# Sharing the second biases of 59 expert visits between TensorE and VectorE, with wider gate operations and an identity product for the residual

## What is computed

```python
xn = layernorm(x)                                    # x: (8, 256, 128)
# attention
Qf, Kf = elu(xn @ Wq) + 1, elu(xn @ Wk) + 1          # 16 heads of 8 features
num = Qf @ (Kf.T @ V);  den = Qf @ sum(Kf) + 1e-6    # V = xn @ Wv, by batch and head
attention = (num / den) @ Wo
# experts
probs = softmax(xn @ gate_w.T + gate_b)              # 8 logits
topk_vals, topk_idx = top_k(probs, 2)
h = relu(xn @ w1[e] + b1[e])                         # 128 -> 256
expert_out = h @ w2[e] + b2[e]                       # 256 -> 128
ffn = sum over the two of topk_vals * expert_out
out = x + attention + ffn
```

## Time and profile before

| | us |
|---|---|
| median of 3 runs (119.38 to 120.27) | 119.73 |
| the profiled execution | 119.96 |
| its span, first to last instruction | 118.2 |
| around the span | 1.76 |
| TensorE busy | 100.9 (85% of the span) |
| VectorE busy | 71.0 (60%) |
| ScalarE busy | 58.4 (49%) |
| GpSimd busy | 50.8 (43%) |

### The profile page before, as it was taken

One profiled execution on the slowest core, in us unless ns is written; L12 is line 12 of the kernel. 1 busy time (PEld: TensorE's weight loads), 2 busy tenths in 40 slices (PEclk: granted clock), 3 DMA queues, 4 the chain that ended last, 5 costly groups with the idle time before them and its releaser, 6 DMA issues.

```text
span 118.2 us, 3075 instructions
## 1 busy us (share of the span) xinstructions
PE 100.9 (85%) x763; PEld 91.3 (77%) x763; DVE 71.0 (60%) x291; ACT 58.4 (49%) x167; POOL 50.8 (43%) x66
## 2 busy tenths in 40 slices
PE   6967989999797897579999999999999899999100
PEld 6935968667676786469999999999999799999100
DVE  0749897998718976320575656557566565574600
ACT  1556996454020111117667676667666476666000
POOL 5004800467777778011001404022514458787870
PEclk9999999999999999967999999999999999999955
DMA  3999000002112116999855655856677758882522
GB/s 94 237 322 392 32 0 6 0 0 72 51 48 72 48 53 153 240 246 377 240 129 134 148 140 152 181 143 133 177 176 153 171 107 185 177 152 22 44 22 25
DMA packets 16656, 15.52 MB, mean 131 GB/s; under 512 B 1920, under 2 KB 16256, under 8 KB 16512
## 3 DMA queue, kind: packets, MB, share of 16 engines
q1 hardware_dynamic: 13248, 12.88, 38.8%
q0 software_dynamic: 2816, 2.18, 11.8%
q10 hardware_dynamic: 576, 0.27, 0.9%
HBM read 12.09 MB, written 3.23 MB: 130 GB/s over the span
## 4 chain that ended last, share of the span: by engine, by line
issue 28%; POOL 19%; PE 19%; DVE 13%; DMA 10%; ACT 2%; SPq 2%; POOLq 2%; DVEq 0%
POOL out L459 19%; DMA x_tok<-in_x 6%; DMA out<-res 5%; PE banks L968 4%; PE banks L937 3%; PE banks L1030 3%; PE banks L990 3%; PE banks L1005 2%; DVE att L766 2%; POOLq L115 2%; DVE rden L762 1%; SPq L354 1%; PE banks L921 1%; DVE idx L634 1%; PE banks L967 1%
## 5 line engine op out<-in xcount | busy, mean ns | idle before, releaser
L547 ACT ACTIVATE h<-banks,w_now 128x128 f32<-128x128 f32 x118 | 36.9, 364 | 19.7 <-PE banks L1061 19.7
L459 POOL DMA_INDIRECT out<-acc,token x16 | 25.0, 1562 | 34.5 <-DVE acc L795 33.3
L1061 PE MATMUL banks<-xsT,w_now 128*128 x236 | 37.5, 283 | 0.1
L1074 PE MATMUL banks<-w_all,h 128*128 x236 | 36.2, 277 | 0.3 <-DVE y L787 0.2
L1061 PEld LDWEIGHTS banks<-xsT,w_now 128*128 128x128 f32 x236 | 31.9, 197 | 0.8 <-issue 0.5
L787 DVE TENSOR_TENSOR y<-banks,w_all 128x128 f32<-128x128 f32 x59 | 17.2, 292 | 24.1 <-PE banks L1074 15.6
L1074 PEld LDWEIGHTS banks<-w_all,h 128*128 128x128 f32 x236 | 30.9, 192 | 1.0 <-issue 0.9
L795 DVE SCALAR_TENSOR_TENSOR acc<-y,xs,acc 128x128 f32 x59 | 20.7, 351 | 0.8 <-DVE y L787 0.5
L444 POOL DMA_INDIRECT sorted_dram<-xrow,slot x16 | 15.8, 990 | 5.3 <-issue 4.6
L893 PE MATMUL banks<-ones 128*128 128x128 f32 x42 | 7.9, 355 | 1.1 <-POOL ones L387 1.1
L893 PEld LDWEIGHTS banks<-ones 128*128 128x128 f32 x42 | 7.4, 265 | 1.5 <-POOL ones L387 1.1
(11 more groups left out here) (97 smaller groups left out, 108.7 us busy)
## 6 DMA issues: line engine op xcount, KB each, us to landing
w_now<-in_w1b SPq DMA_DIRECT2D x59, 129.0 KB, 2.5
w_all<-in_w SPq DMA_DIRECT2D x1, 1536.0 KB, 9.6
out<-res SPq DMA_DIRECT2D x4, 256.0 KB, 5.4
xs<-sorted_dram SPq DMA_DIRECT2D x3, 276.0 KB, 5.4
x_tok<-in_x SPq DMA_DIRECT2D x3, 256.0 KB, 6.6
xs<-sorted_dram SPq DMA_DIRECT2D x2, 138.0 KB, 3.4
x_tok<-in_x SPq DMA_DIRECT2D x2, 128.0 KB, 2.6
sorted_dram<-xrow,slot POOLq DMA_INDIRECT x16, 2.4
```

The lines of the kernel that those rows point to most:

```text
L459: nc.gpsimd.indirect_dma_start(out=out_rows, out_offset=bass.IndirectOffsetOnAxis(ap=token[:, s:s + 1], axis=0), in_=acc[:, s * D:(s + 1) ...
L547: nc.scalar.activation(h[:, i % NH, c, :], h_ps[i % NHP][:, c * P:(c + 1) * P], ACT.Relu, bias=w1_now[:, i % NW, H + c:H + c + 1]).then_in ...
L1061: last = nc.tensor.matmul(h_ps[i % NHP][:, c * P:(c + 1) * P], w1_now[:, i % NW, c * P:(c + 1) * P], xsT[:, bass.ds(toff, P)], start=True, ...
L1074: last = nc.tensor.matmul(y_ps[i % NYP], h[:, i % NH, c, :], w2_all[:, bass.ds(woff + c * D, D)], start=(c == 0), stop=(c == KC - 1))
```

## The change

- Second biases. `bias_by_pe(i)` is true for odd visits and the last four, 31 of 59. In these `second_product` starts with a product of three rows of ones (bf16) with three rows that hold b2 split into three bf16 parts; `take_y` is left out and `accumulate` reads PSUM. Other visits stay as they were. GpSimd makes the three parts (`split_b2`, five operations on 8 partitions), SyncE lays them out.
- Wider operations. Logits are taken for four tiles at a time, the pairs found for tiles 0 to 7, 8 to 11 and 12 to 15 (three groups, not four), the early gates made for eight tiles at once; kf of the first block comes after the first row numbers. The order on TensorE changes with it.
- Residual. `project_out(k)` starts with the product of the identity with x (fp32, 512 columns) into the same bank; ScalarE copies the sum out (`copy_sum`), VectorE's `residual` goes.
- Fillers. Four products stand between the last `project_out` and the first `transpose_rows`; one of the three fillers at the front goes.
- wq and the gate's bias are loaded by SyncE and no longer by ScalarE's queue; b2 is loaded once more by itself.

```diff
+    EARLY, LATE = slice(0, 8), slice(8, T)
+    PAIR_GROUPS = [(0, 8), (8, 12), (12, 16)]
...
+        def bias_by_pe(i):
+
+            return i % 2 == 1 or i >= NI - 4
...
+            sp.dma_start(gate_bias[:], gate_b.partition_broadcast(P)).then_inc(gate_b_in, 16)
+            sp.dma_start(wq_f[:], wq).then_inc(wq_in, 16)
+            sp.dma_start(b2_f[:], b2).then_inc(b2_in, 16)
             sp.dma_start(w2_all[:], w2).then_inc(w2_in, 16)
+            sp.wait_ge(b2_step, 5)
+            for j in range(3):
+                sp.dma_start(b2_split[j:j + 1, :].rearrange("o (e c) -> o e c", c=WROW)[:, :, 0:D],
+                             b2_parts[j][:]).then_inc(b2_placed, 16)
...
+            def split_b2():
+
+                pool.wait_ge(b2_in, 16)
+                nc.gpsimd.tensor_copy(b2_parts[0][:], b2_f[:]).then_inc(b2_step, 1)
...
+            def copy_sum(k):
+
+                act.wait_ge(wo_done, k + 1)
+                nc.scalar.copy(res[:, blk_tiles(k), :], wo_ps[k].rearrange("p (t d) -> p t d", t=4)).then_inc(res_done, 1)
...
+            copy_attT(0)
+            copy_attT(1)
+            copy_sum(0)
+            copy_attT(2)
+            copy_sum(1)
+            copy_attT(3)
+            copy_sum(2)
             copy_xsT(0)
+            copy_sum(3)
...
-            def residual(k):
-                dve.wait_ge(wo_done, k + 1)
-                nc.vector.tensor_tensor(res[:, blk_tiles(k), :], wo_ps[k].rearrange("p (t d) -> p t d", t=4),
-                                        x_tok[:, blk_tiles(k), :], ALU.add).then_inc(res_done, 1)
...
             def accumulate(i, toff, goff):
-                dve.wait_ge(y_done, i + 1)
+                if bias_by_pe(i):
+                    dve.wait_ge(l2_done, i + 1)
+                    share = y_ps[i % NYP]
+                else:
+                    dve.wait_ge(y_done, biases_by_dve(i + 1))
...
-                nc.vector.scalar_tensor_tensor(out=mine, in0=y[:, i % 2, :], scalar=xs[:, bass.ds(goff, 1)], in1=mine,
+                nc.vector.scalar_tensor_tensor(out=mine, in0=share, scalar=xs[:, bass.ds(goff, 1)], in1=mine,
...
             top_two(0)
+            top_two(1)
             take_logits(1)
-            top_two(1)
+            top_two(2)
+            top_two(3)
             find_pair(0)
             take_logits(2)
-            top_two(2)
+            top_two(4)
+            top_two(5)
+            find_pair(1)
+            take_logits(3)
+            top_two(6)
+            top_two(7)
+            find_pair(2)
+            shares()
             choose(0)
-            take_logits(3)
-            top_two(3)
-            find_pair(1)
-            choose(1)
-            take_logits(4)
-            top_two(4)
-            take_logits(5)
-            top_two(5)
-            find_pair(2)
-            take_logits(6)
-            top_two(6)
-            take_logits(7)
-            top_two(7)
-            find_pair(3)
-            shares(0)
-            shares(1)
             late_shift()
-            finish_k(0)
             pair_starts()
             places(1, slice(0, 4))
+            finish_k(0)
+            finish_k(1)
             places(2, slice(4, T))
-            finish_k(1)
             mask_kv(0)
             finish_q(0)
-            choose(2)
-            choose(3)
+            choose(1)
...
-                if i == 0:
+                if i == 0 and not bias_by_pe(0):
                     take_y(0, woffs[0][0])
-                if i + 1 < NI:
+                if i + 1 < NI and not bias_by_pe(i + 1):
                     take_y(i + 1, woffs[(i + 1) // LOADS][(i + 1) % LOADS])
...
+                for i in range(parts_with(4 * k), parts_with(4 * k + 3) + 1):
+                    pe.wait_ge(x_in[i - 1], 16)
+                nc.tensor.matmul(wo_ps[k].rearrange("p (t d) -> p t d", t=4), ident_t[:], x_tok[:, blk_tiles(k), :],
+                                 start=True, stop=False)
                 pe.wait_ge(attT_copied, k + 1)
                 for j in range(4):
                     t = 4 * k + j
                     last = nc.tensor.matmul(wo_ps[k][:, j * P:(j + 1) * P], attT[:, t * P:(t + 1) * P], wo_f[:],
-                                            start=True, stop=True)
+                                            start=False, stop=(j == 3))
                 last.then_inc(wo_done, 1)
...
+                elif bias_by_pe(i - NYP):
+                    pe.wait_ge(acc_done, i - NYP + 1)
                 else:
-                    pe.wait_ge(y_done, i - NYP + 1)
+                    pe.wait_ge(y_done, biases_by_dve(i - NYP + 1))
+                if bias_by_pe(i):
+                    pe.wait_ge(b2_placed, 16 * 3)
+                    nc.tensor.matmul(y_ps[i % NYP], ones_bf[0:3, 0:P], b2_split[:, bass.ds(woff, D)],
+                                     start=True, stop=False)
                 for c in range(KC):
                     last = nc.tensor.matmul(y_ps[i % NYP], h[:, i % NH, c, :],
                                             w2_all[:, bass.ds(woff + c * D, D)],
-                                            start=(c == 0), stop=(c == KC - 1))
+                                            start=(c == 0 and not bias_by_pe(i)), stop=(c == KC - 1))
                 last.then_inc(l2_done, 1)
 
...
-            warm_up(3)
+            warm_up(2)
             project_vg(2)
+            project_vg(3)
             transpose_x(3)
-            project_vg(3)
+            project_vg(4)
             transpose_x(4)
+            project_vg(5)
             rank_rows(0)
-            project_vg(4)
-            rank_rows(1)
-            project_vg(5)
             project_vg(6)
             project_vg(7)
+            rank_rows(1)
             project_k(1)
+            project_q(0)
             rank_rows(2)
-            project_q(0)
-            rank_rows(3)
             project_k(2)
...
+            warm_up(4, residuals=3)
             transpose_rows(0)
             transpose_rows(1)
```

More of the change, by code:

```diff
@@ L129, in linear_attention_with_pair_sorted_experts @@
         wo_f = sb("wo_f", [P, D])
+        b2_f = sb("b2_f", [E, D])
+        b2_rest = sb("b2_rest", [E, D])
+        b2_parts = [sb(f"b2_part{j}", [E, D], BF16) for j in range(3)]
+        b2_split = sb("b2_split", [3, E * WROW], BF16)
         gate_bias = sb("gate_bias", [P, E])
@@ L204, in linear_attention_with_pair_sorted_experts @@
         q_ps = [banks[:, i, :] for i in (2, 3, 4, 0)]
[L205 to L206 removed]
+        vg_four = [banks[:, i:i + 2, 0:R * (D + E)].rearrange("p b (r n) -> p b r n", r=R) for i in (2, 6, 2, 6)]
+        k_ps = [banks[:, i, :].rearrange("p (t d) -> p t d", t=4) for i in (4, 1, 0, 7)]
         rank_ps = banks[:, 5, 0:(T + 1) * NP].rearrange("p (t c) -> p t c", c=NP)
@@ L324, in normalised, with biases_by_dve, pairs_known @@
             return [sum(len(n) for n in norm[:i + 1]) for norm in (NORM_DVE, NORM_ACT, NORM_POOL)]
+        def bias_by_pe(i):
+            return i % 2 == 1 or i >= NI - 4
+        def biases_by_dve(i):
+            return sum(not bias_by_pe(j) for j in range(i))
+        def pairs_known(t):
+            return sum(t >= a for a, _ in PAIR_GROUPS)
         def group_of_visit(i):
@@ L569, in _ @@
             exp_gates(0)
-            exp_gates(1)
             exp_k(0)
-            for b in range(4, 7):
+            for b in range(4, 6):
                 copy_v(b)
             exp_k(1)
+            copy_v(6)
             copy_v(7)
             exp_q(0)
+            exp_gates(1)
             exp_k(2)
-            exp_gates(2)
             exp_q(1)
@@ L582, in _ @@
             exp_q(3)
-            for k in range(NBLK):
-                copy_attT(k)
+            copy_attT(0)
[5 more added lines that the diff above has]
+            copy_sum(2)
             copy_xsT(0)
+            copy_sum(3)
             for i in range(NI):
@@ L865, in _ @@
             dve.wait_ge(w2_in, 16)
-            residual(3)
             dve.wait_ge(acc_set, 1)
@@ L887, in _, with warm_up @@
         def _(pe):
-            def warm_up(times, after=0):
+            def warm_up(times, after=0, residuals=0):
                 pe.wait_ge(ones_set, 1)
@@ L949, in rank_rows @@
                 pe.wait_ge(pair_done, g + 1)
-                nc.tensor.matmul(rank_ps[:, blk_tiles(g), :], before_bf[:], of_pair[:, blk_tiles(g), :],
-                                 start=False, stop=False)
-                for t in range(4 * g, 4 * g + 4):
+                a, b = PAIR_GROUPS[g]
+                nc.tensor.matmul(rank_ps[:, a:b, :], before_bf[:], of_pair[:, a:b, :], start=False, stop=False)
+                for t in range(a, b):
                     last = nc.tensor.matmul(rank_ps[:, t + 1:T + 1, :], ones_bf[:, 0:P],
```

141 lines of the change are left out of this document (74 added, 67 removed).

## The result

The changed kernel takes **125.73 us** (median of four runs, 125.60 to 125.87) against 119.56 (118.56 to 120.27): a ratio of 1.052, 95% interval 1.044 to 1.060. The profiled execution takes 125.86 with a span of 124.0. The forecast was 128.0 in a range from 122.5 to 131.5, and slower with a chance of 0.85.

A forecast was written before the change was run, and what follows sets the result against it. TensorE's gapless stream was taken to bound the expert visits, VectorE and GpSimd the end. Front -0.3, loop +10.2 and end -1.6 sum to +8.3: 128.3 us on the profiled execution, 128.0 as median; range 122.5 to 131.5.

The forecast's parts named there:

- The small product, 0.35 each: Ahead of 31 visits' second products: a three-row product costs TensorE 0.30 us plus 0.053 for its columns, 0.35 in all.
- Rival (a): The small product is nearly free, its weights loaded beside the product before: 0.055 us each, 119.4 us in all; chance 0.09.
- The loop, +10.2: Visits up to 56's second product: 29 small products at 0.35 us lengthen TensorE's stream by 10.2 (7.3 to 12.2), uncovered.
- with nothing in between: In the expert visits before the change: TensorE runs eight records per visit, 0.895 us, without gaps.
- the 0.3 us of waits: Over all visits before the change: TensorE stood still only 0.3 us ahead of second products, 0.2 for VectorE's y.
- VectorE's lost additions as worth nothing in the loop: In the visits: VectorE loses 31 of 59 additions, which gains nothing because VectorE waits for TensorE there.
- The end, -1.6: After visit 56's last column: the last add starts 2.9 us later instead of 4.5, a gain of 1.6 (1.2 to 2.0).
- No longer behind: At the end: with one operation each for visits 55 to 58, VectorE keeps up with TensorE.
- The front, -0.3: Up to the third first product: it starts at 54.2 us instead of 54.48; bounds -1.6 to +1.2.
- Edits at nothing: At the front: the split of b2 and the moved loads of wq and the gate's bias were counted as costing nothing.
- 43.8 was forecast: At the front: the table of offsets is written at 43.8 us, where it was 43.13 before.
- 0.66 was forecast: Ahead of the table: the identity product delays it by 0.86 us, less 0.2 for VectorE's dropped addition of x.

The follow-up runs named there:

- e2: The changed kernel with the small bias product over 128 rows (three parts of b2, the rest zeros) in place of three; 122.40 us.
- e1: The changed kernel with the small products left out, so 31 visits lack their second bias in the result; 120.58 us.
- e3: The changed kernel with all 59 second biases on VectorE, as before the change; 118.37 us, 0.996 of the kernel before.
- e5: The 128-row small-product kernel, with VectorE accumulating a shared visit before it takes the next y; 119.81 us, 1.002 of the kernel before.
- e8: The changed kernel with the loads of wq and the gate's bias back on ScalarE's queue; median 128.81 us, profiled execution 126.86.
- e11: The changed kernel with all biases on VectorE, x added by VectorE and no fillers; 118.28 us, 0.987 of the kernel before.
- e12: The kernel before with the sharing of the biases alone (three-row products, odd visits and last four); 126.65 us, 1.058 of the kernel before.

## Why the forecast was right, and which terms were off

- **The small product, 0.35 each: right.** The one-row rows priced it to the hundredth, and e2 shows that the rows are the cause: 0.107 over 128 rows, 0.35 over three. This agrees with the Trainium skill, "TensorEngine Tiling (Array Packing)", Key Properties, by which a change of mode drains TensorE. Rival (a) needed 0.07 or less.
- **The loop, +10.2: the mechanism right, the term mis-sized; it measured +7.7.** The step that failed is "with nothing in between" and the 0.3 us of waits in the earlier trace rows. Idle time in these rows begins at a record's modelled end, 0.16 behind its last column, so gaps below 0.16 don't show and longer ones look shorter; the 0.42 at 91.77 drawn as no gap shows what that hides. "Perfetto Trace Analysis" of the Trainium skill, in its section on the tensor engine's instructions, warns that this end is a model. Counted by records, 2.6 us were lost, 1.75 of them at reads of offsets and 0.6 at two loads of weights that came late. In the changed kernel 1.0 to 1.35 us of products are queued when a read begins, no visit of the loop waits for its weights, and the loss is gone (0.1).
- **VectorE's lost additions as worth nothing in the loop: right for after, but they are not free.** e1 and e2 show that the shared bank comes free later, which costs 2 to 3 us against e3 as soon as the 0.35 don't cover it; e5 shows that VectorE's order is the reason.
- **The end, -1.6: it measured -1.0.** The lag is 3.43, not 2.9, since GpSimd was still at the add begun at 115.29, and both later adds follow it at 1.87. That add was left out of the sum, and with it what delays it: it waits for visit 54's accumulate, which begins at 114.66 after 0.67 of idle time, behind a read of VectorE's own offsets (0.76 from 113.67 on). "No longer behind" was wrong there: the additions are gone, the reads are not.
- **The front, -0.3: it measured -0.9.** The kernel before was traced once, with its clock down, so what the edits give at an equal clock isn't shown. After the change the clock is 1.00 as forecast, but not by the fillers. "Edits at nothing" failed for the loads: with wq and the gate's bias behind x, x lands in 4.2 us instead of 6.6 (rows below), and the table is 1.06 earlier than in e8. With the loads back it stands at 43.76, where 43.8 was forecast; the identity product delays it by 0.46 to 0.70 in the three pairs of traces with and without it, and 0.66 was forecast. Without identity products and fillers the third first product starts at 52.03 (e11), 2.45 earlier than before; these two give 1.6 of that back. One by one they are worth 1.5 and 1.1 by that start, 1.1 and 0.9 by the medians, so their gains don't add.
- **The total.** The front came 0.6 earlier and the end 0.6 later than forecast. That these two cancel is luck; the 2.5 of the loop remain.

The landing of x, after the change and before (KB each, us):

```profile
x_tok<-in_x SPq DMA_DIRECT2D x3, 256.0 KB, 4.2
x_tok<-in_x SPq DMA_DIRECT2D x3, 256.0 KB, 6.6
```

## What to carry to other kernels

On an engine that bounds a loop, multiply records by their step and compare with the stretch; busy time and waits count from modelled ends and can hide some per cent. A helper product of few rows among full ones is paid three times over here (0.35 against 0.107); fill its operands with zeros to the rows of its neighbours. Where an operation reads a bank directly to save a copy, look at when it now frees that bank, and an earlier start is worth only what the next load behind it in its queue allows.

## What the runs showed of the hardware

- Between fp32 products over 128 rows a bf16 product with 128 columns costs 0.107 us over 128 rows and 0.35 over three.
- TensorE's read of eight offsets takes 0.6 us of its sequencer; at visit 8 it costs nothing in the changed kernel, with 1.25 us of products queued, 0.12 before, with 0.9 queued, and 0.44 in e1, with 0.6 queued (the two steps behind it are 0.455 and 0.208).
- A visit's weights (129 KB) land in sixteen parts. At visit 42 of the kernel before the last came 1.9 us behind the other fifteen (92.07 and 90.16), and TensorE waited for it.
- The granted clock from 50 to 55 us was 0.66 before and 0.69 in e12, which has the old front but for the split of b2, and 1.00 in the twelve other traces. It is at 1.2 GHz from 51.08 on before and from 51.88 on in e12. TensorE's last three pauses ahead of that are 0.77, 0.77 and 1.06 before and 0.77, 0.77 and 1.14 in e12; in e11, where the clock stays up, they are 0.77, 0.77 and 0.83. Why it fell there stays open.
